# Work order ahead of the expert loops of a fused MoE, attention, MoE kernel: splits, shared chunks and first tiles in another sequence

## What is computed

```
x = x + 0.5 * ffn(layernorm(x))      # stage f0
x = x + attention(layernorm(x))      # 16 heads of 128, causal, with biases
x = x + 0.5 * ffn(layernorm(x))      # stage f1, same weights as f0

def ffn(x):                          # 1024 tokens
    g, u = split(x @ shared_gate_up_w.T)                 # 704 + 704 columns
    shared = sigmoid(x @ shared_gate_w.T) * ((silu(g) * u) @ shared_down_w.T)
    top_w, top_i = top_k(softmax(x @ gate_w.T), 2)       # 8 experts, 2 of them for each token
    he = silu(ge) * ue            # per expert: x @ w1[e] gives 176 + 176 columns
    return sum of top_w * (he @ w2[e]) over the two experts + shared
```

## Time and profile before

| what | us |
|---|---|
| median of 3 runs | 537.37 |
| lowest, highest | 536.12, 541.98 |
| the profiled execution | 537.34 |
| its span on the core | 535.5 |
| f0 ahead of its expert loop | about 0 to 59 |
| f0's expert loop | 59 to 109 |
| attention | about 125 to 425 |
| f1 ahead of its expert loop | 425 to 467 |
| f1's expert loop | 467 to 517 |

### The profile page before, as it was taken

The page is one execution under the profiler, slowest core; times in us unless marked ns, Lnnn a source line. Parts: engine busy times, 40 slices in busy tenths (PEclk is TensorE's granted clock), DMA queues, the critical chain, the costliest instruction groups (busy, mean ns, idle before and its releaser), DMA issues.

```text
span 535.5 us, 10473 instructions
## 1 busy us (share of the span) xinstructions
PE 513.4 (96%) x3298; PEld 455.7 (85%) x3299; DVE 337.9 (63%) x867; ACT 269.7 (50%) x731; POOL 274.6 (51%) x364
## 2 busy tenths in 40 slices
PE   8999899988899999999999999999999899999995
PEld 4787799976789898999999989999998788899985
DVE  5689766659754564565545645655548568766647
ACT  4983355531662463553634635536345366355640
POOL 1738877752565470752734707527332131767760
PEclk9999999999999999999999999999999899999999
DMA  8941233353001001010010010100001230222327
GB/s 282 384 161 31 77 103 98 108 168 99 1 20 60 21 2 59 20 57 1 20 59 20 0 59 20 44 15 20 0 2 39 80 119 1 70 90 98 108 90 237
DMA packets 20123, 39.34 MB, mean 73 GB/s; under 512 B 2944, under 2 KB 10496, under 8 KB 20096
## 3 DMA queue, kind: packets, MB, share of 16 engines
q1 hardware_dynamic: 15680, 26.92, 14.9%
q0 software_dynamic: 4416, 12.06, 7.0%
HBM read 29.80 MB, written 9.18 MB: 73 GB/s over the span
## 4 chain that ended last, share of the span: by engine, by line
PE 82%; DVE 10%; ACT 3%; DMA 1%; issue 1%; SPq 1%; POOL 1%; DVEq 0%; ACTq 0%
PE bank L186 19%; PE bank L188 18%; PE bank L187 18%; PE bank L1622 5%; PE bank L1595 5%; PE bank L1604 4%; PE bank L1594 3%; PE bank L1623 3%; PE bank L1081 2%; DVE x_res L927 2%; PE bank L192 1%; DVE bank L712 1%; DMA wd_r<-in_wd 1%; PE bank L193 1%; PE bank L1129 1%
## 5 line engine op out<-in xcount | busy, mean ns | idle before, releaser
L1358 POOL TENSOR_TENSOR s_a<-s_a,rr_a 128x128 f32<-128x128 f32 x64 | 25.8, 403 | 133.7 <-DVE rr_a L1461 133.7
L1405 ACT ACTIVATE s_a<-s_a,mn_a 128x128 f32<-128x128 f32 (+1 forms) x128 | 56.8, 447 | 21.2 <-DVE mn_a L1455 21.0
L1451 DVE SCALAR_TENSOR_TENSOR s_a<-bank,cst 128x384 f32<-128x384 f32 x64 | 35.3, 551 | 33.6 <-PE bank L1595 33.3
L536 POOL DMA_INDIRECT xn<-x_normed,tok_i_f x46 | 45.9, 998 | 14.9 <-issue 10.7
L186 PE MATMUL bank<-xT_h,area_h 128*128 128x512 f32 x124 | 51.2, 413 | 0.7 <-ACT qk_a L1398 0.7
L188 PE MATMUL bank<-xT_h,area_l 128*128 128x512 f32 x124 | 48.5, 391 | 0.0
L187 PE MATMUL bank<-xT_l,area_h 128*128 128x512 f32 x124 | 48.5, 391 | 0.0
L1398 ACT ACTIVATE qk_a<-bank,bias_a 128x512 f32<-128x512 f32 x32 | 21.9, 684 | 50.2 <-PE bank L188 47.7
L1443 DVE TENSOR_SCALAR qk_a<-bank,bias_a 128x512 f32<-128x512 f32 x32 | 24.0, 751 | 36.7 <-PE bank L188 36.7
L1410 ACT ACTIVATE pT_a<-bank 128x384 f32<-128x384 f32 x64 | 30.9, 486 | 28.9 <-PE bank L1604 28.3
L1467 DVE SCALAR_TENSOR_TENSOR area_l<-bank,bias_a,area_h 128x256 fp32r<-128x256 f32 x64 | 30.5, 478 | 20.1 <-ACT area_h L1415 20.1
(11 more groups left out here) (194 smaller groups left out, 1650.3 us busy)
## 6 DMA issues: line engine op xcount, KB each, us to landing
area<-in_wqkv SPq DMA_DIRECT2D x8, 768.0 KB, 4.1
area_r<-in_w SPq DMA_DIRECT2D x16, 256.0 KB, 4.3
xn<-y_by_token SPq DMA_DIRECT2D x12, 256.0 KB, 3.4
w_r<-in_w SPq DMA_DIRECT2D x8, 352.0 KB, 7.5
x_normed<-xn SPq DMA_DIRECT2D x4, 512.0 KB, 5.2
area<-in_wo SPq DMA_DIRECT2D x8, 256.0 KB, 2.6
x_res<-in_x_in SPq DMA_DIRECT2D x4, 256.0 KB, 4.4
wgu_r<-in_wgu SPq DMA_DIRECT2D x4, 256.0 KB, 6.7
```

The lines of the kernel that those rows point to most:

```text
L536: pool.indirect_dma_start(xe[m % XR], None, xd, bass.IndirectOffsetOnAxis(ap=tok_i[:, m:m + 1], axis=0)).then_inc(s_xe[m % XR], 16)
L1405: act.activation(s[b][:, cols], s[b][:, cols], ACT.Exp, bias=mn[:, b, t:t + 1], scale=-1.0, accum_out=rs[:, b, t:t + 1]).then_inc(s_e, 1)
L1451: dve.scalar_tensor_tensor(s[b][:, :], bank[3 + u % 2][:, 0:3 * P], -INV_SCALE, cst[:, C_MASK:C_MASK + 3 * P], ALU.mult, ALU.max).then_inc ...
```

## The change

It touches only orders, with two exceptions (the bank of one product, and the expert list). In f0 and f1 alike:

- TensorE: `shared_up(9)` moves behind `tile_in(0, 0)`. The dummies are 4, behind `tile_in(1, 1)` only. `up(1)` writes bank 5 instead of 3 and waits for the token codes (bank 5 held them) instead of `shared_low(9)`; `tile_in(3)`, `up(2)` and `inner_turn(1)` go ahead of the waits for all w2 splits; `down(0)` comes then, and the wait for `shared_low(9)` stands in front of tile 3's step.
- ScalarE: `shared_high(0)` ahead of `shared_silu(1)`; `tile_high(0)` ahead of `shared_high(8)`; `shared_high(9)` inside the expert loop's third round; the high parts at other places.
- VectorE: `shared_low(0)` ahead of `shared_mul(1)`; `shared_mul(6)` between the first two outputs; `tile_experts` right behind `tokens`; `tile_low(0)`, `tile_low(1)` earlier; `shared_out(3)` and `shared_low(9)` among the first tiles. In f0 it has 12 of the 23 low parts, before 8: it takes 13 and 19 to 22 and gives 8 away.
- GpSimd: low part 2 between the two variances, and none between the one-hot arrays and the first gather.
- `tile_experts` compares with seven of the eight ends, and the reduction writes integers directly; the minimum as an instruction of its own (line 789) goes.

```diff
-ENTRY = {True: (10, 24), False: (0, 8)}
+ENTRY = 4
-POOL_FIRST = {"normed": (2, 3, 5, 6, 7), "assigned": (9, 10, 11), "hot": (12, 13), "gather1": (18,),
-              "gather2": (19,), "gather3": (20, 21, 22)}
-POOL_SECOND = {"normed": (0, 1, 2), "assigned": (3,), "hot": (4, 5)}
-LOWS_FIRST = {"stats1": (1,), "mul0": (4,), "mul6": (8,), "mul7": (14, 15), "mul8": (16,), "out3": (17,)}
-LOWS_SECOND = {"mul7": (6, 7)}
-HIGHS_FIRST = {"turn0": (1, 2), "logits0": (3, 4, 5), "silu0": (6, 7, 8), "turn1": (9,), "silu2": (10,),
-               "logits1": (11, 12), "silu3": (13, 14, 15), "silu5": (16, 17), "high5": (18,), "silu6": (19,),
-               "silu7": (20, 21, 22)}
-HIGHS_SECOND = {"turn1": (0, 1), "logits1": (2, 3), "silu3": (4, 5), "silu5": (6, 7)}
+POOL_FIRST = {"rstd0": (2,), "normed": (3, 5, 6, 7, 8), "assigned": (9, 10), "gather2": (11,), "gather3": (12,),
+              "gather4": (18,)}
+POOL_SECOND = {"normed": (0, 1, 2), "assigned": (3,), "gather3": (4,), "gather4": (5,)}
+LOWS_FIRST = {"stats1": (1,), "xn1": (4,), "tokens": (13, 14, 15, 16), "out2": (17,), "low8": (19, 20), "turn0": (21,),
+              "turn1": (22,)}
+LOWS_SECOND = {"experts": (6, 7)}
+HIGHS_FIRST = {"turn0": (1, 2), "logits0": (3, 4, 5), "silu0": (6,), "high0": (7,), "turn1": (8,), "silu2": (9, 10),
+               "logits1": (11, 12), "silu3": (13, 14), "high5": (15, 16, 17), "silu6": (18,), "silu7": (19,),
+               "high6": (20,), "silu9": (21,), "tile1": (22,)}
+HIGHS_SECOND = {"turn1": (0, 1), "logits1": (2, 3), "silu3": (4, 5), "high5": (6, 7)}
...
+                def up_bank(m):
+                    return bank[5 if m == 1 else 2 + m % 2]
...
                     shared_silu(0)
                     highs("silu0")
+                    shared_high(0)
+                    highs("high0")
                     shared_silu(1)
-                    shared_high(0)
...
                     shared_high(6)
+                    highs("high6")
+                    shared_silu(8)
                     shared_high(7)
-                    shared_silu(8)
+                    tile_high(0, 0)
                     shared_high(8)
                     shared_silu(9)
-                    tile_high(0, 0)
-                    shared_high(9)
+                    highs("silu9")
                     tile_high(1, 1)
+                    highs("tile1")
...
+                        with nc.allow_low_precision(reason="a count of at most seven"):
+                            dve.tensor_reduce(tile_e[0:1, :], tile_cmp[0:1, :, :], op=ALU.add,
+                                              axis=AX.X).then_inc(s_expert, 1)
...
                     norm_apply(dve, n, 1)
+                    lows_of("xn1")
                     shared_mul(0)
-                    lows_of("mul0")
+                    shared_low(0)
                     shared_mul(1)
-                    shared_low(0)
...
                     tiles_of_slots()
-                    for j in range(2):
-                        shared_out(j)
+                    shared_out(0)
+                    shared_mul(6)
+                    shared_out(1)
                     tokens()
-                    shared_mul(6)
-                    lows_of("mul6")
+                    lows_of("tokens")
+                    tile_experts()
+                    lows_of("experts")
+                    shared_low(6)
                     shared_mul(7)
-                    lows_of("mul7")
-                    shared_low(6)
+                    shared_out(2)
+                    lows_of("out2")
+                    shared_mul(8)
                     shared_low(7)
-                    tile_experts()
-                    shared_mul(8)
-                    lows_of("mul8")
-                    shared_out(2)
+                    tile_low(0, 0)
                     shared_low(8)
-                    shared_out(3)
-                    lows_of("out3")
+                    lows_of("low8")
+                    tile_low(1, 1)
                     shared_mul(9)
-                    tile_low(0, 0)
-                    shared_low(9)
...
-                    tile_low(1, 1)
                     inner_mul(0, 0)
+                    lows_of("turn0")
+                    shared_out(3)
+                    tile_low(2, 0)
+                    inner_mul(1, 1, up_bank(1))
+                    inner_low(0, 0)
+                    lows_of("turn1")
+                    shared_low(9)
+                    tile_low(3, 1)
+                    inner_mul(2, 0)
+                    inner_low(1, 1)
...
                     tile_in(0, 0)
-                    keep_warm(pe, 4, ENTRY[first][0])
+                    shared_up(9)
                     pe.wait_ge(s_hl, SC + AHEAD - 1)
                     tile_in(1, 1)
-                    keep_warm(pe, 4, ENTRY[first][1])
+                    keep_warm(pe, 4, ENTRY)
...
                     tile_in(2, 0)
-                    pe.wait_ge(s_hl, SC + AHEAD)
-                    up(1, 1)
+                    pe.wait_ge(s_tok, 1)
+                    up(1, 1, up_bank(1))
                     next_experts(2)
                     inner_turn(0, 0)
+                    tile_in(3, 1)
+                    up(2, 0)
+                    inner_turn(1, 1)
                     pe.wait_ge(s_wh, len(jobs))
                     wait_low(pe, len(jobs) - 1)
                     pe.wait_ge(s_dnv, NT // 2)
-                    step(2, 2, 0, False)
+                    down(0, 0, False)
+                    pe.wait_ge(s_hl, SC + AHEAD)
                     step(3, 3, 1, False)
```

More of the change, by code:

```diff
@@ L516, in run_pool @@
                         norm_rstd(pool, n, 0)
+                        lows_of("rstd0")
                     norm_rstd(pool, n, 1)
@@ L625, in run_act @@
                     shared_silu(5)
-                    highs("silu5")
                     shared_high(5)
@@ L648, in inner_silu @@
                         act.wait_ge(s_eu, m + 1)
-                        act.activation(he[b][:, :], bank[2 + b][:, 0:IM], ACT.Silu).then_inc(s_es, 1)
+                        act.activation(he[b][:, :], up_bank(m)[:, 0:IM], ACT.Silu).then_inc(s_es, 1)
                     def tile_out(m, b):
@@ L660, in run_act @@
                             tile_high(m + 1, (m + 1) % 2)
+                        if m == 2:
+                            shared_high(9)
                         if m < NM:
@@ L1114, in next_experts, with up @@
                         pe.reg_load(e_up, tile_e[0:1, bass.ds(m, 1)])
-                    def up(m, b):
+                    def up(m, b, at=None):
                         e = expert(e_up)
@@ L1121, in up @@
                             part = slice(k * P, (k + 1) * P)
-                            last = split_matmuls(pe, bank[2 + b][:, 0:2 * IM],
+                            last = split_matmuls(pe, (bank[2 + b] if at is None else at)[:, 0:2 * IM],
                                                  (xeT_h[b][:, part], xeT_l[b][:, part]),
```

22 lines of the change are left out of this document (8 added, 14 removed).

## The result

The changed kernel takes 535.58 us (median of 22 executions, 533.61 to 536.86) against 537.08 for the kernel before (22 executions beside it, 535.30 to 541.98): ratio 0.9967, 95% interval 0.9957 to 0.9977. That is 1.5 us, about 0.3% less. The prediction had 4.2 us less, 533.1: right in sign and inside its range, wrong in size. The profiled execution took 535.43 us, its span 533.6 where before had 535.5: 1.9 us.

The account below looks back on a forecast made before the run. TensorE (82% of the chain that ended last) was taken as the bound, with GpSimd a second chain through the expert loop; 3.5 us in the first stage plus 0.7 in the second, off 537.34, gave 533.1 us, range 530.8 to 536.6.

Parts of the forecast that it names:

- Start: First stage, 8 to 41 us: the 0.98 us stall at 21.13 goes, TensorE keeps 0.3 us (bounds 0 and 0.98).
- Up 0 in the first stage: First tile's up product on TensorE, first stage: starts at 54.1 to 54.3 instead of 58.91, 4.7 us earlier.
- Tile 2 behind VectorE's queue: First stage's first tiles: VectorE's queue ahead of tile 2 delays up 2 by about 0.6 us; up 0 to up 3 6.1.
- TensorE's chain as a whole: First expert stage: TensorE's chain 4.1 us shorter (bounds 2.5 and 5.0).
- The cap: End of first stage: GpSimd's 2.4 us plus 1.1 slack at y limit the stage's gain to 3.5 us, not 4.1.
- GpSimd: First stage: scatter 0 and the whole GpSimd chain 2.4 us earlier (bounds 1.7 and 2.8), first gather at 44.2.
- rival B: First-stage cap does not bind and TensorE keeps more: 5.9 us gained, 531.5 us; chance 0.22.
- Second stage: Second expert stage: first tile at 466.5 instead of 467.12; with a smoother pipeline start 0.7 us gained (bounds 0 and 1.4).
- Attention "only shifted": Attention, between the two expert stages: moved in time only, no gain or loss counted.
- rival D: TensorE's clock falls with dummies cut from 34 to 4: slower, 538 to 546 us for three or more spells; chance 0.08.
- rival C: VectorE's lock-out by GpSimd moves: two 2.5 us meetings on low 7 or tile 1, gain 1.7 or less, 535.7; chance 0.22.
- The rule on the port: VectorE splits meeting GpSimd's: at most one split, 1.3 us (1.7 if wide), by the skill's rule; 2.5 by an earlier row.

Follow-up runs that it names:

- e1: Changed kernel with the expert-list wait and two register loads moved ahead of tile 0's turn on TensorE's queue, both stages; 534.22 us.
- e13: Changed kernel with the second up product back in part 9's bank, high 9 and low 9 moved back with it; 536.88 us, ratio 0.9999.
- e12: Changed kernel with only w2 low part 18 moved from GpSimd to VectorE; first-stage slots to silu 22 62.46 us, 62.50 in the changed kernel.
- e4: Changed kernel with tile 0's turn and splits back behind up 9 in both stages; second entry (slot turn to up 0) 13.19 us, 13.40 in the changed kernel.
- e6: Changed kernel with, in the second stage only, tile 0 back behind up 9 and part 7 back early; second entry 12.25 us, 13.40 in the changed kernel.
- e7: Changed kernel with only part 7 (high 7, low 7) moved back early in the second stage; second entry 13.49 us, 13.40 in the changed kernel.
- e5: Changed kernel with w2 low part 17 moved on VectorE from ahead of shared-expert part 7 to behind part 8; 536.05 us.

## Why the prediction was wrong in size

Start: right. The stall at 21 went, and 0.84 us were gained at the slot turn in this pair of profiles. The step left TensorE 0.3 of the 0.98 and brought VectorE's token codes 0.3 us sooner, before the edits behind them; with the scatter of this place (40.6 to 41.9) the difference says little.

Up 0 in the first stage: forecast 54.1 to 54.3, found 55.09. The chain up to it was right to 0.1 to 0.5 us: up 8 went on at 47.16 (forecast 47.7), the second half of up 9 began at 51.53 (51.8), silu 9 ended at 53.82 (53.9). Then I let up 0 follow silu 9 by 0.2 to 0.4 us. It follows by 1.27: **the two register loads, about 0.9 us, were not priced**, because they have no row. e1 settles it. The kernel before could hardly have shown them: in its second stage up 0 follows silu 9's end by 1.30 us (465.82 to the 467.12 of the earlier trace rows), but there VectorE's part of tile 0 came last, ending at 466.87, and the loads lay beside it.

Tile 2 behind VectorE's queue: forecast 0.6 us given back between up 0 and up 3, found 0.92 (5.53 before, 6.45 after), and 0.2 more over the loop. The mechanism was right, the size too small. TensorE's chain as a whole gained 2.7 us in this stage instead of 4.1: the loads' 0.9 and these 0.5. The cap hid that in the forecast, since only 3.5 of the 4.1 were counted. e13 shows what stands on the other side: without the bank another 0.44.

GpSimd: forecast -2.4, measured 65.17 to 62.51, -2.66, and -2.70 at the last scatter. First gather 43.75 (44.2), though it took 1.75 us, not 1.06. Right. The cap of 3.5 never came into force: TensorE gained only 2.7 itself, the first addition followed low 11 without a wait for a DMA, and e12 shows that GpSimd relieved alone changes nothing at tile 22. So the half of rival B that held is that the cap does not bind; its other half, that TensorE keeps 5.9 us, did not. Where TensorE does get further (e1), GpSimd holds it back by 0.6 to 0.7 us.

Second stage: forecast -0.7, found +0.93 at the entry and -0.19 in the tiles. **This is the step that failed**, 1.4 us of the 2.3 that are missing. I counted silu 8's wait (0.75) and silu 9 (0.85) as new and four dummies, a wait of 0.58 and one of 0.3 as gone. The sum itself was wrong: 1.04 us is the time of all eight dummies, and even with 1.04 the terms give 0.3 us less, not the 0.6 of 466.5 for 467.12. With the 0.44 that four dummies fewer made (1.04 to 0.60) they give 0.3 us more. And the overlap was wrong: the dummies and the 0.58 lay beside silu 9, product 9 and VectorE's part of tile 0, so taking them away gave almost nothing (from silu 9's end to up 0 1.30 us before, 1.08 after). The path in before was up 8, up 9, silu 9, product 9, low 0, up 0, and now silu 8's wait and tile 0's turn stand in front of up 9, with the register loads behind silu 9. Also low 6 cannot come earlier, as ScalarE's high 6 waits for the down products in both kernels (456.72, after 4.04 us), while low 7, now behind product 8, comes 3.0 us later. e4, e6 and e7 show that either of the two, the early tile or the late low 7, holds the entry at 13.2 to 13.5.

Attention "only shifted": right, 348.58 in both. The clock (rival D): a fall appeared in the first stage's end (0.50 at 119), which before did not have, behind the same 1.9 us of waiting; by the lengths it cost nothing at the second stage. The entries kept 1.00, with 4 dummies for 34. What I took for a fixed cost of both kernels, the half clock at 419, is a fall that some executions don't have, worth 1.2 to 1.6 us in the profiles.

The sum mended: 0.8 less in the first stage (2.7 for 3.5) and 1.4 less in the second leave 2.0 of the 4.2; the spans say 1.9, the medians 1.5. That the time is the one of rival C (535.7) is luck: one row of over 2 us did stand in front of low 7, but e5 prices it at 0.4 us, not 2.5.

The rule on the port: split 17 met split 11 and took 2.26 us, 1.6 over its own 0.68. The Trainium skill (SBUF — State Buffer, Who interferes with whom) has whoever starts first hold the ports for its whole instruction. A meeting then costs at most the other's one instruction, here 1.70, and this row agrees; e5's 2.17 us are 1.5 over, beside a split of 1.28, so a little more than that; the 2.5 us of the earlier trace rows did not come back. The row of 0.31 us for the reduction beside GpSimd's gathers also agrees with its exemption.

## What to carry to other kernels

Between two rows of an engine there may be work that has no row: register loads stood as 0.9 us of "idle", labelled with an engine that had long been done. Before pricing a path, measure the distance from the last real releaser to the start in every place of the trace that has the same code, and look which other part ended just before it there. When a wait is to be removed, write down the path that remains beside it; two edits that each cover the other's price look harmless singly and must be undone together to be seen. When an edit moves a piece of work, look in its trace where the meeting that it should remove has gone. And where the time between profiles and medians doesn't fit, look at the granted clock behind each gap of TensorE before looking for a cause in the change.

## What the runs showed of the hardware

- Two loads of a register from SBUF on TensorE's queue took about 0.9 us (e1: 1.27 to 0.36 us between silu 9 and up 0; the entries 0.83 and 0.73 shorter).
- The granted clock fell to 0.50 behind a gap of 1.57 us in 12 of 15 profiles; with 11 dummies leaving 0.28 us of the gap it stayed at 1.00 in all three. The stretch with the fall was 1.2 to 1.6 us longer. A fall behind an earlier gap of 1.92 us made no difference in the lengths, where VectorE was 0.85 to 1.00 busy; the medians leave that open.
- A gather's instruction on GpSimd that started beside a VectorE split already under way took 1.75 us (43.75) and 2.09 (454.82), instead of 0.95. Where the gather had started first (457.96 in before, the split at 458.27) it took 1.06.
